# Second half of the expert's first layer with the weights stationary, in a gated cross-attention and mixture-of-experts kernel

## What is computed

```python
def _L0_ffn_ref(x, W1, b1, W2, b2, Wa, Wb):
    pooled = x.mean(axis=1)
    h = jnp.tanh(pooled @ W1 + b1)
    probs = jax.nn.softmax(h @ W2 + b2, axis=-1)
    top_p, top_i = jax.lax.top_k(probs, 3)
    top_w = top_p / top_p.sum(axis=-1, keepdims=True)
    w = jnp.einsum('bk,bke->be', top_w, jax.nn.one_hot(top_i, 8))
    for e in range(8):
        z = jax.nn.gelu(x @ Wa[e]) @ Wb[e]       # 256 -> 1024 -> 256
        zone_outputs = zone_outputs + z * w[:, e, None, None]
    return x + zone_outputs
x = x + jnp.tanh(g_xattn[0]) * _L0_xattn_ref(_layernorm(x), ctx, ctx, mask, ...)
x = x + jnp.tanh(g_ffn[0]) * _L0_ffn_ref(_layernorm(x), ...)
```

## Time and profile before

| | |
|---|---|
| median of 3 runs | 451.78 us (449.39 to 452.66) |
| the profiled execution | 449.78 us, of it 448.0 us span from the first to the last instruction |
| PE busy | 366.3 us, 82% of the span |
| PEld busy | 280.3 us, 63% |
| DVE, ACT, POOL busy | 187.1, 193.7, 160.5 us |
| granted TensorE clock, mean | 0.909 of full speed |
| last stage | 294 to 448 us |

### The profile page before, as it was taken

One profiled execution on the slowest core, in us unless ns is written; L12 is line 12 of the kernel. 1 busy time (PEld: TensorE's weight loads), 2 busy tenths in 40 slices (PEclk: granted clock), 3 DMA queues, 4 the chain that ended last, 5 costly groups with the idle time before them and its releaser, 6 DMA issues.

```text
span 448.0 us, 8681 instructions
## 1 busy us (share of the span) xinstructions
PE 366.3 (82%) x3044; PEld 280.3 (63%) x3044; DVE 187.1 (42%) x560; ACT 193.7 (43%) x398; POOL 160.5 (36%) x219
## 2 busy tenths in 40 slices
PE   2714689859679697699698868589999999999996
PEld 2413356637457475476476656458877788888885
DVE  4202633725726738537458446323332412222222
ACT  2310453634355455356264546543346343444331
POOL 4840672842536734645638558710000000000000
PEclk9955887988969999889699889969999999999999
DMA  5642454542545536355336342210101001011000
GB/s 142 221 108 82 125 148 112 151 122 83 152 125 149 150 107 157 105 153 160 109 98 169 111 124 79 80 31 12 32 22 31 11 23 33 1 33 32 0 12 12
DMA packets 31769, 40.40 MB, mean 90 GB/s; under 512 B 8840, under 2 KB 25536, under 8 KB 31728
## 3 DMA queue, kind: packets, MB, share of 16 engines
q1 hardware_dynamic: 25024, 22.07, 17.2%
q0 software_dynamic: 4784, 16.98, 13.1%
q10 hardware_dynamic: 1920, 0.79, 0.7%
HBM read 33.09 MB, written 6.74 MB: 89 GB/s over the span
## 4 chain that ended last, share of the span: by engine, by line
PE 51%; DMA 24%; POOL 8%; SPq 7%; DVE 5%; issue 3%; ACT 2%; ACTq 0%; POOLq 0%; DVEq 0%
PE bank L1140 14%; PE bank L1168 14%; DMA kst<-k_scr 8%; DMA xr<-in_x 6%; DMA k_scr<-k_hl 5%; PE bank L1150 4%; SPq L301 4%; PE bank L1006 4%; DMA r_scr<-xr 4%; PE bank L998 3%; POOL wa L442 3%; PE bank L1023 2%; PE bank L946 2%; SPq L307 2%; DMA ctx_s<-in_ctx 2%
## 5 line engine op out<-in xcount | busy, mean ns | idle before, releaser
L736 DVE CUSTOM_DVE_ANT_0 bank<-bank,maskb 112x375 f32<-112x375 f32 x128 | 67.8, 568 | 43.7 <-PE bank L946 43.4
L522 ACT ACTIVATE pT<-bank 125x448 f32<-125x448 f32 x96 | 49.4, 539 | 57.6 <-PE bank L966 57.3
L946 PE MATMUL bank<-kst,qbd 128*112 128x375 f16 x128 | 39.8, 375 | 40.7 <-DMA kst<-k_scr 26.7
L1140 PE MATMUL bank<-wa,ctxT 128*112 x288 | 72.2, 388 | 0.0
L899 DVE SCALAR_TENSOR_TENSOR stage<-bank,wbc,stage 128x448 f16<-128x448 f32 x48 | 32.8, 684 | 87.1 <-ACT stage L700 87.1
L1168 PE MATMUL bank<-wb,stage 128*112 x576 | 67.0, 273 | 1.2 <-DVE stage L899 1.2
L1168 PEld LDWEIGHTS bank<-wb,stage 128*112 128x112 f16 x576 | 63.4, 130 | 4.2 <-issue 1.4
L700 ACT ACTIVATE stage<-bank,wbc 128x448 f16<-128x448 f32 x48 | 30.2, 631 | 54.1 <-PE bank L1150 54.1
L442 POOL TENSOR_TENSOR wa<-stage,wa 128x512 f16<-128x512 f32 x32 | 36.7, 1156 | 45.4 <-ACT wa L618 45.2
L437 POOL TENSOR_SCALAR stage<-stage 128x512 f32<-128x512 f32 x64 | 39.2, 625 | 36.2 <-DMA stage<-in_L_ffn_Wa 21.8
L956 PE MATMUL bank<-ident_b,maskb 112*128 112x448 bf16 (+1 forms) x96 | 37.2, 388 | 16.8 <-ACT pT L522 16.8
(11 more groups left out here) (116 smaller groups left out, 456.4 us busy)
## 6 DMA issues: line engine op xcount, KB each, us to landing
stage<-in_L_ffn_Wa POOLq DMA_DIRECT2D x16, 512.0 KB, 7.3
stage<-in_L_ffn_Wb POOLq DMA_DIRECT2D x16, 512.0 KB, 7.5
kst<-k_scr SPq DMA_DIRECT2D x32, 187.5 KB
ctx_s<-in_ctx SPq DMA_DIRECT2D x8, 375.0 KB
k_scr<-k_hl SPq DMA_DIRECT2D x16, 187.5 KB
qbd<-q_scr SPq DMA_DIRECT2D x32, 56.0 KB
xa<-in_x SPq DMA_DIRECT2D x8, 112.0 KB, 9.3
q_scr<-q_hl SPq DMA_DIRECT2D x32, 28.0 KB
```

What stands on the lines that cost most here:

```text
L522: a.activation(pT[:, t % PRING, :], bank[0:CK, ST_BANKS[t % len(ST_BANKS)], 0:QUAD], ACT.Exp).then_inc(s["act_exp"], 1)
L736: v.tensor_tensor_reduce(out=bank[0:SQ, e, 0:SK], in0=bank[0:SQ, e, 0:SK], in1=maskb[:, b % 2, 0:SK], scale=-1.0, scalar=3.0e38, op0=ALU.a ...
L946: T.matmul(bank[0:SQ, e, 0:SK], qbd[:, b % 2, e, p, :], kst[:, b % 2, p * SK:(p + 1) * SK], start=True, stop=True).then_inc(s["pe_s1"], 1)
L1140: ins = T.matmul(o, x2b[:, b % 2, xs * DT * SQ + t * SQ:xs * DT * SQ + (t + 1) * SQ], wa[:, bass.ds(e * (4 * CHUNK) + ws * (2 * CHUNK) + t ...
```

## The change

The first half of the first layer stays as it was (6 wide matmuls into bank 0, GELU, 4 transposes into bank 2). The second half is computed the other way round: 128 columns of the weights are the stationary operand (128 x 128) and the 112 tokens move. The result has the hidden features on partitions at once and needs no transposes: 4 tiles x 2 feature tiles x 3 = 24 *narrow* matmuls a use, into bank 1 or 3 in turn. They are written in turn with the wide ones, three narrow and one wide, six times, and then six narrow ones. Its GELU (`gelu_w`) is 128 x 448 into a new buffer `h_w`, from which ACT makes the high part (`hi_w`) and DVE the low part (`low`). `hT` has two copies, for even and odd uses. `g2` begins with the tiles of the second half, which is ready a turn ahead, and then takes those of the transposed one.

```diff
+            def gelu_w(u):
+                act.wait_ge(s["g1w_done"], u + 1)
+                need(act, s["low_done"], u)
+                a.activation(h_w[:, :], bank[:, 1 + 2 * (u % 2), 0:QUAD], ACT.Gelu_apprx_tanh, scale=1.0 / WSCALE).then_inc(s["geluw_done"], 1)
...
+            def hi_w(u):
+                act.wait_ge(s["wbc_done"], 1 if u // TOPK < ROUTES[1][0] else 2)
+                act.wait_ge(s["geluw_done"], u + 1)
+                need(act, s["g2_done"], u - 1)
+                a.activation(hT[:, u % 2, QUAD:2 * QUAD], h_w[:, :], ACT.Copy, scale=wbc[:, u:u + 1]).then_inc(s["hiw_done"], 1)
...
-            gelu(0, 0)
-            gelu(0, 1)
+            gelu(0)
+            gelu_w(0)
+            hi_w(0)
             for u in range(B * TOPK):
-                for hf in range(2):
-                    ht_hi(u, hf)
-                    if u + 1 < B * TOPK:
-                        gelu(u + 1, hf)
+                hi_0(u)
+                if u + 1 < B * TOPK:
+                    gelu(u + 1)
+                    gelu_w(u + 1)
+                    hi_w(u + 1)
...
+            def low(u):
+                dve.wait_ge(s["wbc_done"], 1 if u // TOPK < ROUTES[1][0] else 2)
+                dve.wait_ge(s["hiw_done"], u + 1)
+                v.scalar_tensor_tensor(out=hT[:, u % 2, 3 * QUAD:4 * QUAD], in0=h_w[:, :], scalar=wbc[:, u:u + 1],
+                                       in1=hT[:, u % 2, QUAD:2 * QUAD], op0=ALU.mult, op1=ALU.subtract).then_inc(s["low_done"], 1)
...
-            def g1(u, e, hf):
+            def g1(u, e):
...
+                wide = [(t, xs, ws) for t in range(DT) for xs, ws in ((0, 0), (0, 1), (1, 0))]
+                for i in range(4 * DT):
+                    f, t = i // DT, i % DT
+                    for xs, ws in ((0, 0), (1, 0), (0, 1)):
+                        ins = T.matmul(bank[:, 1 + 2 * (u % 2), f * SQ:(f + 1) * SQ],
+                                       wa[:, bass.ds(e * (4 * CHUNK) + ws * (2 * CHUNK) + t * CHUNK + 512 + f * 128, 128)], x_part(u, xs, t),
+                                       start=(t == 0 and xs == 0 and ws == 0), stop=(t == DT - 1 and ws == 1))
+                    if i == 4 * DT - 1:
+                        ins.then_inc(s["g1w_done"], 1)
+                    if i < len(wide):
+                        if i == 0:
+                            need(pe, s["gelu_done"], u)
+                        tw, xs, ws = wide[i]
+                        ins = T.matmul(bank[0:SQ, 0, :], x_part(u, xs, tw),
+                                       wa[:, bass.ds(e * (4 * CHUNK) + ws * (2 * CHUNK) + tw * CHUNK, 512)],
+                                       start=(i == 0), stop=(i == len(wide) - 1))
+                        if i == len(wide) - 1:
+                            ins.then_inc(s["g1_done"], 1)
...
-                for f in range(FT):
-                    if f % 4 == 0:
-                        pe.wait_ge(s["htlo_done"], u * 2 + f // 4 + 1)
+                for i in range(FT):
+                    f = (i + 4) % FT
+                    if i % 4 == 0:
+                        pe.wait_ge(s["lo0_done" if i else "low_done"], u + 1)
...
-                ht(u, 0)
+                ht(u)
                 if nxt is not None:
-                    g1(u + 1, nxt, 0)
-                ht(u, 1)
-                if nxt is not None:
-                    g1(u + 1, nxt, 1)
+                    g1(u + 1, nxt)
```

More of the change, by code:

```diff
@@ L230, in flamingo_layer @@
         rb = [xa[:], kst_flat[0:SQ, 2 * FF + 4 * D:2 * FF + 6 * D].bitcast(F32)]
-        hT = stage[:].rearrange("p a f -> p (a f)")[:, 0:FT * SQ].bitcast(F16)
+        hT = stage[:].rearrange("p a f -> p (a f)")[:, 0:2 * FT * SQ].bitcast(F16).rearrange("p (a f) -> p a f", a=2)
+        h_w = kst_flat[:, 2 * FF + 6 * D:2 * FF + 6 * D + 2 * QUAD].bitcast(F32)
         bank = stack.enter_context(nc.psum_tensor("bank", [128, 8, 512], F32))
@@ L243, in flamingo_layer @@
                  "h_act lg_done nmx_done e_done idx_done wdiag_done wbc_done idx_loaded "
[L244 removed]
+                 "g1_done g1w_done gelu_done geluw_done ht_full hi0_done hiw_done lo0_done low_done g2_done y_done r_loaded0 r_loaded1 x2b_loaded0 x2b_loaded1 out_written0 out_written1").split()
         s = {n: sem(n) for n in names}
@@ L686, in _, with gelu @@
                 normed2(o)
[L688 to L701, removed]
+            def gelu(u):
+                act.wait_ge(s["g1_done"], u + 1)
+                need(act, s["ht_full"], u)
+                a.activation(h_f[:, 0:512], bank[0:SQ, 0, :], ACT.Gelu_apprx_tanh, scale=1.0 / WSCALE).then_inc(s["gelu_done"], 1)
@@ L703, in _, with hi_0 @@
+            def hi_0(u):
+                act.wait_ge(s["ht_full"], u + 1)
+                a.activation(hT[:, u % 2, 0:QUAD], bank[:, 2, 0:QUAD], ACT.Copy, scale=wbc[:, u:u + 1]).then_inc(s["hi0_done"], 1)
             o_copy(B - 1)
             act.wait_ge(s["lo_done"], NPART)
-            gelu(0, 0)
-            gelu(0, 1)
+            gelu(0)
+            gelu_w(0)
+            hi_w(0)
             for u in range(B * TOPK):
-                for hf in range(2):
-                    ht_hi(u, hf)
-                    if u + 1 < B * TOPK:
-                        gelu(u + 1, hf)
+                hi_0(u)
[3 more added lines that the diff above has]
+                    hi_w(u + 1)
@@ L891, in _ @@
                     route_shares(0)
+            def low(u):
[3 more added lines that the diff above has]
+                                       in1=hT[:, u % 2, QUAD:2 * QUAD], op0=ALU.mult, op1=ALU.subtract).then_inc(s["low_done"], 1)
             for u in range(B * TOPK):
                 b, k = u // TOPK, u % TOPK
[L895 to L901, removed]
+                if u == 0:
+                    low(0)
+                dve.wait_ge(s["hi0_done"], u + 1)
+                v.scalar_tensor_tensor(out=hT[:, u % 2, 2 * QUAD:3 * QUAD], in0=bank[:, 2, 0:QUAD], scalar=wbc[:, u:u + 1],
+                                       in1=hT[:, u % 2, 0:QUAD], op0=ALU.mult, op1=ALU.subtract).then_inc(s["lo0_done"], 1)
+                if u + 1 < B * TOPK:
+                    low(u + 1)
                 if u == 0:
@@ L1128, in zone, with x_part @@
                 return pe.value_load(idx_row[0:1, u:u + 1], min_val=0, max_val=NZ - 1)
-            def g1(u, e, hf):
+            def x_part(u, xs, t):
+                return x2b[:, (u // TOPK) % 2, xs * DT * SQ + t * SQ:xs * DT * SQ + (t + 1) * SQ]
+            def g1(u, e):
                 b, k = u // TOPK, u % TOPK
-                if k == 0 and hf == 0:
+                if k == 0:
                     pe.wait_ge(x2b_loaded[b % 2], 16 * (b // 2) + 16)
[L1135 to L1144, removed]
@@ L1146, in ht @@
-            def ht(u, hf):
-                pe.wait_ge(s["gelu_done"], u * 2 + hf + 1)
-                need(pe, s["htlo_done"], u * 2 - 1 + hf)
+                need(pe, s["geluw_done"], u - 1)
+                if u < 2:
+                    pe.wait_ge(s["dve_max"] if u == 0 else s["act_exp"], s1_no(B, 0, 0) if u == 0 else tile(B, 0, 0))
+                wide = [(t, xs, ws) for t in range(DT) for xs, ws in ((0, 0), (0, 1), (1, 0))]
[16 more added lines that the diff above has]
+                            ins.then_inc(s["g1_done"], 1)
@@ L1149, in ht @@
+            def ht(u):
+                pe.wait_ge(s["gelu_done"], u + 1)
+                need(pe, s["lo0_done"], u)
                 for f in range(4):
-                    ins = T.transpose(bank[:, 2 + hf, f * SQ:(f + 1) * SQ], h_f[:, hf * 512 + f * 128:hf * 512 + (f + 1) * 128],
-                                      ident[0:SQ, 0:SQ])
+                    ins = T.transpose(bank[:, 2, f * SQ:(f + 1) * SQ], h_f[:, f * 128:(f + 1) * 128], ident[0:SQ, 0:SQ])
                 ins.then_inc(s["ht_full"], 1)
@@ L1163, in g2 @@
                 o = bank[0:SQ, 4 + b % 2, 0:D]
-                for f in range(FT):
-                    if f % 4 == 0:
-                        pe.wait_ge(s["htlo_done"], u * 2 + f // 4 + 1)
+                for i in range(FT):
+                    f = (i + 4) % FT
+                    if i % 4 == 0:
+                        pe.wait_ge(s["lo0_done" if i else "low_done"], u + 1)
                     for hs, ws in ((0, 0), (0, 1), (1, 0)):
-                        ins = T.matmul(o, hT[:, hs * FT * SQ + f * SQ:hs * FT * SQ + (f + 1) * SQ],
+                        ins = T.matmul(o, hT[:, u % 2, hs * FT * SQ + f * SQ:hs * FT * SQ + (f + 1) * SQ],
                                        wb[:, bass.ds(e * (4 * CHUNK) + ws * (2 * CHUNK) + f * D, D)],
-                                       start=(k == 0 and f == 0 and hs == 0 and ws == 0), stop=(k == TOPK - 1 and f == FT - 1 and hs == 1))
+                                       start=(k == 0 and i == 0 and hs == 0 and ws == 0), stop=(k == TOPK - 1 and i == FT - 1 and hs == 1))
                 ins.then_inc(s["g2_done"], 1)
             e = zone(0)
-            g1(0, e, 0)
-            g1(0, e, 1)
+            g1(0, e)
```

## The result

| | before | after |
|---|---|---|
| first medians | 451.92 us (4 runs) | 436.13 us (4 runs, 434.9 to 437.43) |
| profiled execution | 449.78 us, span 448.0 | 437.43 us, span 435.6 |
| ratio after / before | | 0.9678, 95% interval 0.9622 to 0.9733 |
| again, six runs beside 17 of before | 449.4 us | 436.05 us; ratio 0.9705 (0.9665 to 0.9745) |

Two differences have to be kept apart: that between the two profiled executions is 12.35 us, that between the first medians 15.8. With 17 runs of before the second shrinks to 13.4, since the four first runs of before lay high (449.39 to 452.66, against 444.92 to 451.71 for the 17). The forecast had 8.9. So something like 3.5 to 4.5 us of real gain is missing from my sum.

What follows compares the result with a forecast made beforehand. TensorE's array was taken as the bound of the last stage; turns -11.0, start +1.7 and +1.7 and end -1.3 sum to -8.9 us, from 451.78 to a forecast of 442.9 us, range 438 to 452.

Steps and rivals of the forecast that it cites:

- The turn: TensorE's period in the last stage falls from 5.99 to 5.51 us; over 23 turns -11.0 us.
- Rivals 1 and 3: Narrow matmuls paced by weight loads, 470 or 460 us, chance 0.09; switching between narrow and wide costs, 452 to 454, 0.07.
- The end: In the last turn, half of the second layer runs before the wait for the low part: -1.3 us.
- The start: Before the last stage's first transposes: an idle gap of the array, +1.7 us, and a clock fall after it, +1.7 us.
- Its first half: At the last stage's start, the array idles for the GELU table load and GELU before the first transposes: +1.7 us.
- Its second half: After the start's idle gap of some 1.8 us, the clock runs 3.4 us at half: +1.7 us.
- The base: The saving was taken from the median of the runs, 451.78 us, not the profiled execution's 449.78.
- The sequencer: TensorE's register instructions take 5.3 us a turn against 5.51 on the array, so costed at nothing.
- Rival 2: The sequencer becomes the bound in the last stage's turns, each matmul costing it some time: 446.5 to 452 us, chance 0.12.
- The slack of ACT and DVE: In the last stage's turns, their GELU and high and low parts are ready before TensorE needs them: no cost.

Runs made afterwards that it cites:

- the fixed-address run: The changed kernel with expert 0's weights at fixed addresses in both layers for every use, so no register instructions for addresses: 436.81 us, ratio 0.9723.
- the doubled load: The changed kernel with the next expert's number read into a register twice in each turn: 449.21 us, ratio 0.9991.
- the unmixed kernel: The changed kernel with each turn's six wide matmuls first and the 24 narrow ones behind them: 437.11 us, ratio 0.9731.

## Why the prediction was wrong

**The turn: right.** -11.0 forecast, -11.5 measured over the stretch. The narrow matmul costs the 49 ns of the earlier trace rows, the wide one behind it the few ns I gave it. What was gained beyond the forecast is in the turns with the `TAIL` steps. The Trainium skill's figure of about 81 ns for a sustained pair (TensorE: Matmul & The Clock Gate, Back-to-back issue gap) isn't borne out here: 49 ns over 48 pairs with 112 moving columns, and 89 ns only where register instructions stood between them. Rivals 1 and 3 fall with that.

**The end: right.** -1.3 forecast, -1.4 measured; the old order of the second layer gives it back.

**The start: the step that failed**, by 2.8 us: +3.4 forecast, +0.6 measured between the two profiled executions. Its first half, "+1.7 us" for the gap behind the wide product, holds only where the clock is at half during the whole of `g1(0)`: the fixed-address run, whose array work is the same, took 6.45 us to its transposes, 1.54 more than before. But I took the level of the clock from one trace. In thirteen traces the clock rose between 1.5 and 4.9 us after the stage's first matmul, and before's 4.6 was at the late end. With an early rise the changed kernel needs 5.1 to 5.5 us. How long before would have needed then, no trace shows. An estimate: at 427 ns each its sixth wide matmul ended 2.56 us into the stage, and the transposes came 2.35 us after that, at 4.91. Had the clock risen at 2.3 us, that matmul would have ended at 2.4, the transposes would have come at 4.75 to 4.8, and the change would cost 0.7. So little of the +0.6 is luck with the clock, but the first half of the term is worth anything from some +0.7 to +1.5 us, as the clock of the execution happens to rise.

Its second half, the fall of the clock at "+1.7 us", was simply wrong: no trace with a gap of 1.5 to 1.7 us at this place has it, one with 4.74 us does, and nothing between was tried. The two gaps of attention that I compared, 1.49 and 1.77 us, give no length from which the clock falls. The trace of the changed kernel has the same gap of 1.49 us at the same place as the earlier trace rows, and there the clock did fall, about 2 us behind it (a line of its timeline and two windows):

```profile
113.44 0.87 PE L962 MATMUL bank<-kst,qbd 128*112 128x375 f16 x2 [1.49 <-DVE negmax L746]
113.60:115.30 1.70, 1.56 (x11) 1.13 (x11) 1.37 (x6) 0.34 (x1) 1.42 (x3) 1.00 0.28 74
115.60:118.80 3.20, 3.20 (x14) 1.96 (x13) 1.91 (x8) 1.05 (x3) 2.88 (x5) 0.50 0.59 146
```

One length, two outcomes: the length alone doesn't decide, and what does, these runs don't show. I took the worse of two ends on the strength of one row.

**The base: the second step that failed.** I carried the saving over to 451.78, a median of three runs. Later medians of before are 449.4, 449.5 and 448.4, so the base was 2.4 us too high. With turns, end and start as the two profiled executions have them, -11.5 - 1.4 + 0.6 = -12.3, which is their difference; from 451.78 that gives 439.5, still inside the range. It took both, the start and the base, to bring the time under 438. What lies between 12.3 and the 13.4 of the larger sample, about 1 us, is inside its interval, and I can't place it.

**The sequencer: right in its conclusion, mis-sized in its term.** I costed it at nothing, and the fixed-address run shows that it costs nothing. But "5.3 us" was about 5.5, by the doubled load and by the sum of the spacings with their longer steps: the 4% by which I had it faster than the array are none. It still stands 1.7 to 1.8 us ahead of the array in the late turns, by the measure used for the unmixed kernel, and that distance neither grows nor goes. The doubled load costs its full 0.65 us. Rival 2 was nearer than its chance said, by a cause that I hadn't named: not a price for each matmul, but longer steps now and then among the register instructions.

**The slack of ACT and DVE: right.** From the first transposes on, TensorE waits for ACT once, at the first transposes themselves (1.73 us), and 0.2 us for DVE at the end.

## What to carry to other kernels

A matmul's price on the array is only half of a trade between few wide and many narrow ones: count the register instructions that each address brings, sum their spacings with the longer steps among them, and check the sum with a version in which the sequencer is surely the bound. The spacing of an instruction that runs once a turn doesn't tell it, since that follows the array while the array is the bound. Here the two periods were within some 0.02 us of each other, and one more load in the turn gave the whole gain back. Where a term rests on the clock's level at one place, look at several executions before it gets a sign, and carry the saving over from an execution to a median only if the median has enough runs.

## Of the hardware, unexpected

- 48 pairs of a 128-column weight load (98 ns shown) and a 112-column matmul ran at 49 ns a pair, and a 112-column load behind a 49 ns matmul delayed the wide one by at most a few ns.
- TensorE's sequencer showed one register instruction each 0.112 or 0.124 us whatever matmuls lay between, and an extra 0.03 to 0.15 us at about every eighth, 0.32 us in a turn of 5.5; the cause of the extra is not known.
- A gap of 1.5 to 1.7 us at the start of the stage left the clock at full in all five traces that have it, one of 4.74 was followed by 3.4 us at half. In attention one and the same gap of 1.49 us was followed by full clock in the trace of before and by half in that of the changed kernel. The clock's rise after the stage's begin varied from 1.5 to 4.9 us between executions.
